# Two expert layers around a linear attention: attention batch by batch, routing of the first batch between the units of the second

## The reference

```
x = x + 0.5 * ffn(layernorm(x))
x = x + attn(layernorm(x))
x = x + 0.5 * ffn(layernorm(x))
```

```
logits = x @ gate_w.T                       # 32 per token
w = softmax(logits) at the top 4, divided by their sum
large = sum over the 4 experts e:        w_e * (silu(x Wg_e) * (x Wu_e)) Wd_e      # 96 wide
small = sum over the same experts' e//2: w_e * (silu(x cWg_c) * (x cWu_c)) cWd_c   # 128 wide, 16 of them
ffn = large + 0.05 * small
```

```
q, k, v = x wq.T, x wk.T, x wv.T ; q, k = rope(q), rope(k)
o_i = sum over j <= i of exp(-lambda_h (i - j)) (q_i . k_j) v_j
attn = concat(o of all heads) wo.T
```

## Time and profile before

| | us |
|---|---|
| median of 3 runs (592.13 to 601.65) | 596.48 |
| the profiled execution | 596.83 |
| its span in the profile | 595.1 |
| TensorE busy | 507.6 (85%) |
| TensorE weight loads busy | 439.8 (74%) |
| VectorE busy | 318.7 (54%) |
| GpSimd busy | 257.4 (43%) |
| ScalarE busy | 142.8 (24%) |

### The profile page before, as it was taken

The page is one execution under the profiler, slowest core; times in us unless marked ns, Lnnn a source line. Parts: engine busy times, 40 slices in busy tenths (PEclk is TensorE's granted clock), DMA queues, the critical chain, the costliest instruction groups (busy, mean ns, idle before and its releaser), DMA issues.

```text
span 595.1 us, 9863 instructions
## 1 busy us (share of the span) xinstructions
PE 507.6 (85%) x3276; PEld 439.8 (74%) x3276; DVE 318.7 (54%) x997; ACT 142.8 (24%) x382; POOL 257.4 (43%) x280
## 2 busy tenths in 40 slices
PE   8589979999039999999999999999858999999900
PEld 7489968887017888889888988888758898888600
DVE  6844333343296647664766476666785444444325
ACT  4102212222234231222132212211420222222211
POOL 0045656663236444434443444333103566666322
PEclk9789999999559999999999999999976999999955
DMA  7989987781650010121012011110295425778173
GB/s 228 322 261 330 331 319 245 257 287 55 236 192 18 28 36 19 54 56 23 31 40 68 19 36 36 52 37 10 86 381 179 154 94 182 234 251 281 55 256 118
DMA packets 46654, 87.79 MB, mean 148 GB/s; under 512 B 6528, under 2 KB 27264, under 8 KB 46592
## 3 DMA queue, kind: packets, MB, share of 16 engines
q1 hardware_dynamic: 37376, 66.05, 34.0%
q0 software_dynamic: 6912, 18.88, 9.4%
q10 hardware_dynamic: 2304, 2.10, 1.0%
HBM read 74.42 MB, written 12.58 MB: 146 GB/s over the span
## 4 chain that ended last, share of the span: by engine, by line
PE 60%; DVE 22%; DMA 11%; issue 3%; SPq 2%; ACT 1%; POOL 1%; POOLq 0%; DVEq 0%; ACTq 0%
PE bank L1180 10%; PE bank L1089 8%; PE bank L1084 7%; PE bank L1217 6%; DMA w_down_sb<-w_down 4%; PE bank L1108 4%; PE bank L1110 4%; PE bank L1193 4%; DVE shared L921 3%; DVE shared L922 3%; DVE shared L920 3%; DMA shared<-z_dram 3%; PE bank L1214 3%; PE bank L1171 3%; PE bank L1199 2%
## 5 line engine op out<-in xcount | busy, mean ns | idle before, releaser
L458 POOL DMA_INDIRECT decay_all<-xn_dram,ids x72 | 69.6, 966 | 121.0 <-PE bank L1056 52.8
L526 POOL TENSOR_TENSOR shared<-shared 128x512 f32<-128x512 f32 x36 | 45.8, 1273 | 130.2 <-DVE shared L922 130.2
L860 DVE COPY oT_all<-bank 128x256 f32<-128x256 f32 x72 | 30.6, 425 | 131.0 <-PE bank L1056 131.0
L467 POOL DMA_INDIRECT z_dram<-probs_all,dest x72 | 70.2, 975 | 36.4 <-ACT probs_all L642 32.7
L1180 PE MATMUL bank<-split_sb 128*128 128x512 f32 x240 | 65.2, 407 | 1.9 <-ACT split_sb L601 0.9
L1089 PE MATMUL bank<-w_ch_sb,oT_all 128*128 128x256 f32 x256 | 65.7, 379 | 0.0
L941 DVE TENSOR_TENSOR split_sb<-bank,split_sb 128x512 fp32r<-128x512 f32 x32 | 22.1, 692 | 66.2 <-ACT split_sb L690 66.2
L634 ACT ACTIVATE rot<-bank 128x224 f32<-128x224 f32 x72 | 25.7, 357 | 132.2 <-PE bank L1089 132.2
L1084 PE MATMUL bank<-w_exp_sb,oT_all 128*128 128x192 f32 x256 | 53.4, 331 | 2.9 <-issue 1.6
L1231 PE MATMUL bank<-split_sb 128*128 128x256 f32 x384 | 53.4, 288 | 1.5 <-DVE split_sb L941 1.5
L1084 PEld LDWEIGHTS bank<-w_exp_sb,oT_all 128*128 128x128 f32 x256 | 43.8, 189 | 10.3 <-issue 5.5
(11 more groups left out here) (141 smaller groups left out, 971.3 us busy)
## 6 DMA issues: line engine op xcount, KB each, us to landing
shared<-w_up_piece SPq DMA_DIRECT2D x32, 448.0 KB, 6.3
w_exp_sb<-w_exp SPq DMA_DIRECT2D x32, 384.0 KB, 8.3
shared<-w_down_piece SPq DMA_DIRECT2D x32, 256.0 KB, 4.3
w_ch_sb<-w_ch SPq DMA_DIRECT2D x16, 384.0 KB, 5.9
shared<-z_dram SPq DMA_DIRECT2D x12, 512.0 KB, 7.1
decay_all<-decay SPq DMA_DIRECT2D x16, 256.0 KB, 2.7
w_down_sb<-w_down SPq DMA_DIRECT2D x16, 192.0 KB, 7.8
xn_dram<-xn_sb ACTq DMA_DIRECT2D x16, 128.0 KB, 6.1
```

The costliest lines, as they stand in the source:

```text
L458: pool.indirect_dma_start(out=xg[s], out_offset=None, in_=xn_dram[l][:, :], in_offset=bass.IndirectOffsetOnAxis(ap=ids[:, SEQ[t]:SEQ[t] + ...
L467: pool.indirect_dma_start(out=z_dram[l][:, :], out_offset=bass.IndirectOffsetOnAxis(ap=dest[:, SEQ[t]:SEQ[t] + 1], axis=0), in_=y_sb[s], i ...
L526: nc.gpsimd.tensor_tensor(dst, rope_a[r % 2], rope_b[r % 2], ALU.add).then_inc(roped, 1)
```

## The change

The units are numbered the other way round: unit n has batch n // 16 and head n % 16. All units of batch 0 come first. Four units share a key and value head of one batch (8 such groups, GS), and each unit loads and splits its own query and output weights, so that these are loaded and split once per batch. Keys and values lie in smaller buffers, and no longer in `xn_sb`. Every group of four units has the projections for the next group behind its units 1 (values), 2 (keys) and 3 (transposition).

When batch 0 is finished (unit 16), its four tiles are copied out, normalised, transposed, multiplied with the gate, and their top 4 taken, one step of one tile in a unit, in units 17 to 29. After the attention the norm, the transposes and the routing start at tile 4. The member table of tiles 0 to 3 is made behind the last split of an output. The logits of layer 1 lie in PSUM banks 2 to 5.

```diff
-        UNITS, GU = H * B, GROUPS * B
+        UNITS, GS = H * B, HKV * B
         def projections(n, place):
-            g, m = n // GU, n % GU
+            G, m = n // GROUPS, n % GROUPS
             if n < 0:
-                return [("q", 0, 0), ("k", 0, 0), ("v", 0, 0), ("v", 0, 1), ("k", 0, 1), ("t", 0, 0)]
+                return [("q", 0), ("k", 0), ("v", 0), ("t", 0)]
             if place == "scores":
-                return [("q", n + 1, (n + 1) % B)] if n + 1 < UNITS else []
-            if g + 1 < HKV and m >= 2:
-                return [("vvkktt"[m - 2], g + 1, m % 2)]
-            return [("t", 0, 1)] if n == 0 else []
+                return [("q", n + 1)] if n + 1 < UNITS else []
+            return [("vkt"[m - 1], G + 1)] if m >= 1 and G + 1 < GS else []
         def splits(n):
             if n < 0:
-                return [("q", 0), ("k", 0)]
-            found = [("o", n // 2)] if n % 2 == 0 else [("q", (n + 3) // 2)] if n + 3 < UNITS else []
-            if n == 0:
-                found.append(("q", 1))
-            if n % GU == 3 and n // GU + 1 < HKV:
-                found.append(("k", n // GU + 1))
+                return [("q", 0), ("k", 0), ("q", 1)]
+            found = [("o", n)]
+            if n + 2 < UNITS:
+                found.append(("q", n + 2))
+            if n % GROUPS == 1 and n // GROUPS + 1 < GS:
+                found.append(("k", n // GROUPS + 1))
             return found
...
+        OUT_AT, STATS_AT, NORM_AT, TURN_AT, COPY_AT, LOGIT_AT, TOP_AT = [H + a for a in (1, 2, 3, 4, 5, 6, 7)]
+        def early_tile(n, first):
+            i = (n - first) // 2
+            return [i] if (n - first) % 2 == 0 and 0 <= i < SB else []
...
SyncE:
             load_results(sp, 0, first_loads)
-            for h in range(1, H):
-                load_head(h)
-                if h % GROUPS == 1 and h // GROUPS + 1 < HKV:
-                    load_kv(h // GROUPS + 1)
+            load_o(0)
+            load_decay(1)
+            load_q(2)
+            load_kv(1)
+            for n in range(UNITS):
+                if n + 3 < UNITS:
+                    load_q(n + 3)
+                if n + 1 < UNITS:
+                    load_o(n + 1)
+                if n + 2 < UNITS:
+                    load_decay(n + 2)
+                if n % GROUPS == 3 and n // GROUPS + 2 < GS:
+                    load_kv(n // GROUPS + 2)
...
ScalarE, in unit n:
-                if n == UNITS - 1:
-                    for i in range(SB):
-                        residual_out(i)
+                for i in early_tile(n, NORM_AT):
+                    root(act_e, 2, i)
+                for i in early_tile(n, COPY_AT):
+                    transposed(act_e, 2, i, early_xT_ps)
                 act_e.wait_ge(pv_mm, n + 1)
                 if n >= 2:
                     act_e.wait_ge(wo_mm, n - 1)
                 nc.scalar.activation(oT_hi[n % 2], o_ps[:, :], ACT.Copy).then_inc(o_copied, 1)
+                if n in (OUT_AT, OUT_AT + 1):
+                    for i in range(2):
+                        residual_out(2 * (n - OUT_AT) + i)
...
VectorE:
+        def early_stats(dve, link, i):
+            dve.wait_ge(x2_copied, i + 1)
+            link(nc.vector.bn_stats(stats[:, i % 2, :], x_sb[:, i, :]))
+            link(nc.vector.bn_aggr(mv[:, i, :], stats[:, i % 2, :]))
+            link(nc.vector.tensor_scalar_add(var_eps[:, i:i + 1], mv[:, i, 1:2], EPS))
+            nc.vector.reciprocal(rvar[:, i:i + 1], var_eps[:, i:i + 1]).then_inc(rvar_ready, 1)
...
in unit n:
                 mask(n, 1)
                 for p in projections(n, "behind"):
                     rotate(p)
-            return lambda: split_output(UNITS - 1)
+                for i in early_tile(n, STATS_AT):
+                    early_stats(dve, link, i)
+                for i in early_tile(n, NORM_AT):
+                    normalise(dve, 2, i)
+                for i in early_tile(n, TOP_AT):
+                    top_values(dve, 1, i)
+                    top_index(dve, 1, i)
+            split_output(UNITS - 1)
...
behind the attention:
-            split_last = attention_dve(dve)
-            norm_dve(dve, tick, 2, split_last)
+            attention_dve(dve, link)
+            members(dve, link, 1, 0, SB)
+            norm_dve(dve, tick, 2, SB)
             route_dve(dve, tick, link, 1)
...
TensorE, in unit n:
                     output(n - 1)
                 for p in projections(n, "behind"):
                     project(p)
+                for i in early_tile(n, TURN_AT):
+                    pe.wait_ge(x2_copied, 2 if i == 0 else SB)
+                    pe.wait_ge(xnT_copied, 2 * TT + i)
+                    transpose_tile(pe, 2, i, early_xT_ps)
+                for i in early_tile(n, LOGIT_AT):
+                    pe.wait_ge(x2_copied, SB)
+                    logits(pe, 1, i)
                 products(n)
```

More of the change, by code:

```diff
@@ L202, in macaron_kernel @@
         xT_ps = [bank[0], bank[1]]
-        logit_ps = [bank[2 + i % 6] for i in range(TT)]
+        logit_ps = [[bank[2 + i % 6][:, 0:E] for i in range(TT)],
+                    [bank[5][:, i * E:(i + 1) * E] for i in range(SB)] + [bank[a][:, 0:E] for a in (2, 3)]
+                    + [bank[5][:, SB * E:(SB + 1) * E], bank[4][:, 0:E]]]
+        early_xT_ps = bank[4][:, 0:D]
         rank_ps, ids_ps, grain_ps = bank[3], bank[5], bank[6]
@@ L607, in norm_act @@
                     scale_results(act_e, 0, i)
-            for i in range(TT):
+            lag = 2 if s >= 1 else 1
+            for i in range(first, TT):
                 n = s * TT + i
@@ L611, in norm_act @@
                     scale_results(act_e, 0, i + 3)
-                act_e.wait_ge(rvar_ready, n + 1)
-                nc.scalar.activation(rstd[:, i:i + 1], rvar[:, i:i + 1], ACT.Sqrt).then_inc(rstd_ready, 1)
-                if i == 2 and beside:
-                    beside()
-                lag = 2 if s >= 1 else 1
-                if i >= lag:
-                    transposed(i - lag)
+                root(act_e, s, i)
+                if i - lag >= first:
+                    transposed(act_e, s, i - lag, xT_ps[(n - lag) % 2][:, 0:D])
                 if s == 1 and i == TT - 3:
@@ L717, in stats_of @@
             def stats_of(i):
-                if 0 <= i < TT:
+                if first <= i < TT:
                     if s == 0:
@@ L737, in inverse @@
             def inverse(i):
-                if 0 <= i < TT:
+                if first <= i < TT:
                     after(("eps", i))
                     nc.vector.reciprocal(rvar[:, i:i + 1], var_eps[:, i:i + 1]).then_inc(rvar_ready, 1)
-            for i in range(-1, TT + 2):
-                if i == 2 and beside:
-                    beside()
+            for i in range(first - 1, TT + 2):
                 add(i + 1, 0)
@@ L751, in norm_dve @@
                 inverse(i - 1)
-                if 0 <= i - 2:
+                if first <= i - 2:
                     normalise(dve, s, i - 2)
@@ L763, in normalise, with members, top_values @@
                                     ALU.subtract, ALU.mult).then_inc(xn_ready, 1)
+        def members(dve, link, l, a, b):
+            dve.wait_ge(index_ready, l * TT + b)
+            link(nc.vector.tensor_copy(ixf[:, a:b, :], top_ix[:, a:b, 0:TOP_K]))
+            link(nc.vector.tensor_tensor(chosen[:, a:b], iota_e.unsqueeze(1).unsqueeze(1).broadcast_to([P, b - a, TOP_K, E]),
+                                         ixf[:, a:b, :].unsqueeze(3).broadcast_to([P, b - a, TOP_K, E]), ALU.is_equal))
+            for h in range(2):
+                ins = nc.vector.tensor_tensor(member2[:, h, a:b, :], chosen[:, a:b, 2 * h, :], chosen[:, a:b, 2 * h + 1, :], ALU.add)
+            link(ins)
+            return nc.vector.tensor_tensor(member[:, a:b, :], member2[:, 0, a:b, :], member2[:, 1, a:b, :], ALU.add)
+        def top_values(dve, l, i):
+            dve.wait_ge(logits_mm, l * TT + i + 1)
+            nc.vector.max(top[:, i, :], logit_ps[l][i]).then_inc(top_ready, 1)
         def route_dve(dve, tick, link, l):
+            first = l * SB
             if l == 0:
@@ L1222, in output @@
             def output(n):
-                h = n // B
-                key = ("o", h)
+                key = ("o", n)
                 pe.wait_ge(w_split, split_order.index(key) + 1)
```

251 lines of the change are left out of this document (118 added, 133 removed).

## The result

| | before | after |
|---|---|---|
| median of the runs, us | 596.32 (592.13 to 601.65, 4 runs) | 614.39 (613.21 to 615.24, 4 runs) |
| the profiled execution, us | 596.83 | 613.21 |

A forecast was written before the change was run, and what follows sets the result against it. TensorE's order of work was taken to bound the attention, with GpSimd's splits joining the path. Terms +12.7 + 0.5 + 1.1 + 0.3 + 0.2 - 2.0 = +12.8 on 596.83 gave 609.6, said as 609 us; range 602 to 615.

The forecast's parts named there:

- the ring: Attention units: cycle TensorE, VectorE, GpSimd, TensorE through two weight splits, 7.39 us, lengthening plain and transposing units; costs 9.3 us.
- Weight splits: Every attention unit loads and splits its own weights: loads free, one more GpSimd split per unit, on the path.
- TensorE's new waits for the early work: Attention units: TensorE's added waits name work of earlier units, so they cost nothing.
- second rival: Attention units: cycle 0.1 to 0.3 us longer on 16 units, from later GpSimd start or slower splits; 611 to 614, chance 0.1.
- Batch order: Attention units: one value projection, key projection and transposition, formerly ahead of or in unit 0, lengthen units; 3.3 us.
- Ahead of unit 0: Before the first attention unit: an earlier GpSimd split delays TensorE's first projection; +0.5 us (0 to 0.7).
- Early work in units 22 and 26: Key-projecting, TensorE-bound attention units: added transposes and gate products cost 2 x 0.54 = +1.1 us.
- VectorE's statistics in unit 18: Attention unit 18: small linked operations of the early norm delay the next rotation; +0.3 us (0 to 0.9).
- The port collision: Attention units 19 and 23: VectorE's normalisation may hold up GpSimd through a shared port pair; 0.2 us in all.
- After the attention: Last attention product to first expert product: fewer normalisations, shorter queue, smaller member step; -2.0 us (-0.9 to -3.6).
- the ring does not bind: Rival for the attention units: TensorE does not wait for the second split, added splits fit GpSimd's idle time; 600.2, chance 0.13.
- the tail pays: Rival for the stretch after the attention: it shortens by 11 us instead of 2, giving 600.6; chance 0.03.

The follow-up runs named there:

- no_early: splits_ahead with filler products ahead of the first key transposition, and batch 0's norm, transposes, gate and top 4 moved back behind the attention; ratio 1.005 to the kernel before.
- ahead_busy: splits_ahead plus products nobody reads in TensorE's idle time, 12 ahead of the first key transposition, 14 behind the attention's last product; ratio 1.005 to the kernel before.
- three_waits: Changed kernel with the wait for the copy of xn dropped from query and key projections in the units, leaving three waits; ratio 1.023 to the kernel before.
- q_first: Changed kernel with the query weight's split listed ahead of the output weight's; ratio 1.009 to the kernel before.
- splits_ahead: Changed kernel with GpSimd doing both weight splits of a unit before its rotated add, order kept; ratio 1.006 to the kernel before.
- batch_early: ahead_busy with three waits, and the first query and key projections started between the norm's tiles; ratio 1.006 to the kernel before.
- before_late_q: Kernel before with query weights split in even units, behind the output weight's split, straight ahead of use, no work added; ratio 1.008 to the kernel before.

## Why the prediction was wrong

The bound, the mechanism and the sign were right. What failed is the size of three terms of the sum, above all the last leg of the ring, from the second split to TensorE's product: 0.83 us in the sum, 0.99 in the changed kernel.

- **Weight splits, the ring: right in kind, too short.** I took "0.83 to TensorE" from unit 0 of the kernel before. In the changed program it is 0.99, with a fourth wait on the product, which the sum does not have; I had put TensorE's new waits for the early work at "nothing" and did not look at this one. On 16 steps that is 2.4 us: the steps from Q(0) to Q(30) without new work beside them are 7.53 to 7.57, not 7.39, but for unit 0 (7.69, in part at the lower clock) and unit 3 (7.63). This is the largest miss. Four lengths of the ring in five kernels (7.54, 7.38, 6.87, none) show the mechanism. My second rival had the length of 0.1 to 0.3 us, by other causes (a later start of GpSimd, slower splits); GpSimd's rows in a plain unit, at +5.88 and 0.73 long, refute those, though the time fell in its range: that was luck, not its mechanism.
- **Batch order, 3.3 us of moved projections: right.** no_early gives 2.55 with 0.76 won in unit 0.
- **Ahead of unit 0: said +0.5, was +1.5.** I wrote that the projections taken away "give no more". The first projection did start later, by 0.77, as said (0.69). But the projections taken away did cost: they had filled the wait for the key rotation. With the hole came the 1.2 GHz level, and 1.2 us, most of it between the first projection and Q(0): 9.89 us, against 8.79 in ahead_busy and three_waits. Where the clock stayed up, in ahead_busy and three_waits, the stretch is 29.66 and 29.70, 0.3 over before.
- **Early work in units 22 and 26: said 2 x 0.54, was 2 x 0.66.** Unit 22's key projection to the next query is the second pair here (the first row, 368.58, is its query):

```profile
368.58 1.62 PE L1222 MATMUL bank<-split_sb 128*128 128x512 f32 x6
372.40 1.66 PE L1222 MATMUL bank<-split_sb 128*128 128x512 f32 x6
377.32 1.63 PE L1222 MATMUL bank<-split_sb 128*128 128x512 f32 x6
```

  That is 3.82 + 4.92 us, where other key units have 3.82 + 4.25. In units 20, 24 and 28 nothing was to be paid, as said.
- **VectorE's statistics in unit 18: said +0.3, was +0.2.** They delay the next rotation, and so the step of unit 19: 7.71 against 7.54.
- **The port collision: said 0.2, was nothing that can be seen.** In unit 19 (Q = 344.88), VectorE's normalisation, then GpSimd's add and scaling beside it:

```profile
349.84 0.46 DVE L790 TENSOR_SCALAR xn_sb<-x_sb,mv,rstd 128x256 f32<-128x256 f32 x1 [0.39 <-ACT rstd L610]
```

```profile
348.88 1.27 POOL L544 TENSOR_TENSOR shared<-shared 128x512 f32<-128x512 f32 x1 [3.11 <-DVE shared L954]
350.23 0.73 POOL L550 TENSOR_TENSOR state_sb<-shared,decay_all 128x256 f32<-128x256 f32 x1
```

  GpSimd's add starts at +4.00 and not +3.84 before the normalisation begins, so all of the 0.17 us of this step is the late rotation; unit 23 takes 7.54. GpSimd's two instructions are as long as ever. The rule of the Trainium skill ("SBUF — State Buffer", Who interferes with whom), by which whoever comes second is fully blocked, would have cost these units 0.8 us, as I worked it out. The rows do not agree with it: the normalisation begins 0.31 us before the end of the add and takes 0.46 us, where 0.40 alone and a full block would make 0.71. It is slowed a little and not blocked, as far as GpSimd's spans, which are rough, can tell.
- **After the attention: said -2.0, was -0.7.** I took half a microsecond off for a shorter queue on ScalarE and TensorE. With the work of tiles 0 to 3 gone, TensorE idled instead and the steps of the four that stay got longer at the lower clock. Only 0.37 of the 0.7 lies ahead of the member table; the rest is in rank and slots, where no line changes, and q_first, splits_ahead and three_waits, with the same tail, have 32.36 to 32.50, nothing under before. With the clock held up the tail is 31.03, 1.4 under before: two thirds of the forecast.

By stretches: forecast 0.5 + 14.3 - 2.0, measured 1.5 + 16.7 - 0.7. The three large misses have one sign, so they did not cancel, and the 614.4 us lie near the top of the range. The rival "the ring does not bind" is refuted by the plain steps alone, "the tail pays" by a tail 0.7 us shorter.

**Left open:** number or order of waits behind the 0.16 us, and why the clock did not fall in three_waits. A version with the ring gone, fillers and three waits, without the early projections, was not run. I expect it at about the 1.005 of ahead_busy, since its queries no longer wait for a split: batch_early, which has three waits, needs 239.69 us for the units and ahead_busy 239.72.

## What to carry to other kernels

Draw the cycle from one engine's step to its next through every in-order queue on the way, and add up the times between starts, with each wait that its last instruction carries: work that is free on an idle engine costs its full time when it stands ahead of what the cycle needs (here 0.68 us a unit in the ring for each split, gone by a changed order in GpSimd's list). Before work off the critical path is taken from TensorE, ask how long TensorE would then idle, and price what follows at the lower clock too. Work moved into an earlier stage is paid there at that stage's bound: here 1.8 us in the units for at most 1.6 in the tail, filler included.

## What the runs showed of the hardware that was not expected

- A product whose split had just ended started 0.99 us behind the split's start with four waits, and 0.83 with three, in the plain units of two kernels each (after and q_first; three_waits and before_late_q).
- After 2.64 us without work TensorE went on at 1.2 GHz in the changed kernel (0.50 in the window from 192 to 194 us), but stayed at a granted clock of 1.00 after a hole of the same 2.64 us in three_waits.
- A GpSimd subtraction of 128 x 256 took 0.73 us alone (263.42 in the changed kernel) and 0.91 beside VectorE's additions to x (178.83 in batch_early; the same line, L466).
